# Macaron block on one core: expert weights loaded into the place of their remainders, four row-pair buffers, and norms that keep their intermediates in PSUM

## What is computed

```
x = x + 0.5 * ffn(layernorm(x))          # part 1
x = x + attn(layernorm(x))               # part 2
x = x + 0.5 * ffn(layernorm(x))          # part 3

ffn(x):  logits = x @ W_gate + b_gate;  top 2 of 8 experts
         y = mean over the two of relu(x @ W_e[e] + b_e[e])
attn(x): q, k, v = split(clip(x @ Wqkv.T, -8, 8));  q, k = layer_norm(q), layer_norm(k)
         softmax(q k' / 4 + slopes * distance, causal) @ v @ Wout.T
```

## Time and profile before

| what | value |
|---|---|
| median of three runs | 1060.15 us |
| the profiled execution | 1064.33 us, of which the span of its trace is 1062.6 us |
| PE busy in the span | 876.8 us (83%) |
| DVE busy | 652.9 us (61%) |
| ACT busy | 446.5 us (42%) |
| POOL busy | 352.6 us (33%) |
| moved by DMA | 162.08 MB, 153 GB/s on average |

### The profile page before, as it was taken

One profiled execution on the slowest core, in us unless ns is written; L12 is line 12 of the kernel. 1 busy time (PEld: TensorE's weight loads), 2 busy tenths in 40 slices (PEclk: granted clock), 3 DMA queues, 4 the chain that ended last, 5 costly groups with the idle time before them and its releaser, 6 DMA issues. The chain is left out here.

```text
span 1062.6 us, 20207 instructions
## 1 busy us (share of the span) xinstructions
PE 876.8 (83%) x6688; PEld 646.4 (61%) x6689; DVE 652.9 (61%) x1296; ACT 446.5 (42%) x818; POOL 352.6 (33%) x342
## 2 busy tenths in 40 slices
PE   2667699994698888858999999999859974699994
PEld 2556588873576776635555555555447763588873
DVE  6647244431988887757777777777427667344432
ACT  2332233331244343335777777777723430133321
POOL 4550577764022122120000000000024440577764
PEclk9997799997799999967999999999978995799998
DMA  8784578773244479664666666655148872378773
GB/s 247 268 276 119 165 142 153 140 134 50 82 152 150 154 194 207 179 203 103 145 134 140 132 138 133 140 132 112 33 140 264 292 246 99 85 142 154 135 136 52
DMA packets 112859, 162.08 MB, mean 153 GB/s; under 512 B 16864, under 2 KB 74336, under 8 KB 112512
## 3 DMA queue, kind: packets, MB, share of 16 engines
q1 hardware_dynamic: 94928, 123.85, 42.4%
q0 software_dynamic: 17856, 37.25, 19.1%
HBM read 97.44 MB, written 67.37 MB: 155 GB/s over the span
## 5 line engine op out<-in xcount | busy, mean ns | idle before, releaser
L827 DVE TENSOR_REDUCE att_part<-att_s_ps 128x2 f32<-128x1024 f32 (+2 forms) x160 | 195.4, 1225 | 61.4 <-PE att_s_ps L675 60.9
L789 ACT ACTIVATE att_prob<-att_st_ps 128x512 f32<-128x512 f32 x320 | 173.7, 595 | 78.7 <-PE att_st_ps L701 78.7
L143 PE MATMUL exp_z_ps<-ex_w_hi,exp_xT_hi 128*128 x312 | 131.7, 422 | 2.3 <-issue 1.0
L145 PE MATMUL exp_z_ps<-ex_w_hi,exp_xT_lo 128*128 x312 | 125.7, 403 | 0.0
L144 PE MATMUL exp_z_ps<-ex_w_lo,exp_xT_hi 128*128 x312 | 125.3, 402 | 0.0
L1470 DVE TENSOR_TENSOR exp_xT_lo<-exp_t_ps,exp_xT_hi 128x512 fp32r<-128x512 f32 x78 | 53.9, 692 | 106.7 <-ACT exp_xT_hi L1456 106.7
L1463 ACT ACTIVATE exp_y<-exp_y 128x512 f32<-128x512 f32 x72 | 45.5, 632 | 171.8 <-DVE exp_y L1482 171.8
L1099 POOL TENSOR_TENSOR ex_w_lo<-ex_bias,ex_w_hi 128x1024 fp32r<-128x1024 f32 x32 | 77.0, 2409 | 92.6 <-ACT ex_w_hi L1203 92.4
L1398 POOL DMA_INDIRECT exp_xg<-xn,ex_token_of x78 | 78.2, 1002 | 88.1 <-SPq L1370 60.4
L714 PE MATMUL att_pv_ps<-att_prob,att_v_sb 128*32 128x256 f32 (+2 forms) x1280 | 101.4, 391 | 1.8 <-ACT att_oT L794 1.8
L639 POOL CAST att_m_parts<-att_part 128x28 fp32r<-128x28 f32 x32 | 6.6, 208 | 271.3 <-DVE att_part L831 271.3
(11 more groups left out here) (199 smaller groups left out, 1713.4 us busy)
## 6 DMA issues: line engine op xcount, KB each, us to landing
ex_bias<-in_L_ffn_W_e SPq DMA_DIRECT2D x32, 512.0 KB, 6.8
v_vals<-st_vals SPq DMA_DIRECT2D x16, 512.0 KB, 2.8
...
```

The costliest lines, as they stand in the source:

```text
L143: nc.tensor.matmul(out, x_hi[:, s], w_hi(c), start=(c == 0), stop=False)
L145: last = nc.tensor.matmul(out, x_lo[:, s], w_hi(c), start=False, stop=(c == C - 1))
L789: nc.scalar.activation(prob[n % 2][:, col:col + 512], st_ps[(e + half) % 3][:, :], ACT.Exp).then_inc(exp_done, 1)
L827: nc.vector.tensor_reduce(out, src, X_AXIS, ALU.max, negate=True).then_inc(red_done, 1)
```

## The change

- `load_weights` now writes each piece straight into its place in `ex.w_lo`. ACT rounds from there into `ex.w_hi`, and POOL subtracts in place. There are eight semaphores for the pieces; piece n waits only for ACT to have rounded piece n-8.
- The memory of the two stage buffers becomes two more row-pair buffers (`XR = 4`). Row pair u waits for pair u-4 to be normed and stored. The turned q/k/v weight uses the first two of them, and waits for their rows instead of for POOL.
- SP issues row pairs two ahead and weights up to two pieces further ahead than before.
- ACT rounds the last piece after the last two tiles' copies, not between them and the ones before. POOL subtracts the last piece only once `picked_done` is there, that is after the top-2 selection.
- `rsqrt_steps` keeps its two intermediates in PSUM (`route_ps` in the routes, a bank of its own, `root_ps`, in the q/k/v block) and forms each Newton step as `(v*y)*(-0.5)*y`, so that no operation of it has two inputs in SBUF.

```
 def rsqrt_steps(nc, chain, var, y, bank):
+    n = var.shape[-1]
+    v, t = bank[:, 0:n], bank[:, n:2 * n]
+    chain(nc.vector.tensor_scalar(v, var, EPS, None, ALU.add))
+    chain(nc.vector.tensor_scalar(y.bitcast(I32), v.bitcast(I32), -0.5, 1597463007.0, ALU.mult, ALU.add))
     for _ in range(3):
-        chain(nc.vector.tensor_tensor(tmp[0], y, y, ALU.mult))
-        chain(nc.vector.scalar_tensor_tensor(tmp[0], tmp[0], -0.5, tmp[1], ALU.mult, ALU.mult))
-        chain(nc.vector.scalar_tensor_tensor(y, tmp[0], 1.5, y, ALU.add, ALU.mult))
+        chain(nc.vector.tensor_tensor(t, v, y, ALU.mult))
+        chain(nc.vector.scalar_tensor_tensor(t, t, -0.5, y, ALU.mult, ALU.mult))
+        chain(nc.vector.scalar_tensor_tensor(y, t, 1.5, y, ALU.add, ALU.mult))
...
             def load_x(u):
-                p = u % 2
-                if u >= 2:
-                    sp.wait_ge(xn_done, 2 * u - 2)
-                    sp.wait_ge(x_stored[p], 16 * (u // 2))
+                if u >= XR:
+                    sp.wait_ge(xn_done, 2 * (u - XR) + 2)
+                    sp.wait_ge(x_stored[u % XR], 16 * (u // XR))
...
             def load_weights(n):
-                if n >= 2:
-                    sp.wait_ge(w_lo_done, n - 1)
-                sp.dma_start(w_stage[n % 2][:, :, :], w_e[n // 2, :, :]...
+                if n >= WR:
+                    sp.wait_ge(w_hi_done, n - WR + 1)
+                sp.dma_start(ex.w_lo[:, 2 * n:2 * n + 2, :].bitcast(F32), w_e[n // 2, :, :]...
...
             for n in range(TILES):
                 pool.wait_ge(w_hi_done, n + 1)
-                nc.gpsimd.tensor_tensor(ex.w_lo[:, 2 * n:2 * n + 2, :], w_stage[n % 2][:, :, :],
+                if n == TILES - 1:
+                    pool.wait_ge(picked_done, 1)
+                nc.gpsimd.tensor_tensor(ex.w_lo[:, 2 * n:2 * n + 2, :], ex.w_lo[:, 2 * n:2 * n + 2, :].bitcast(F32),
...
-                if u < PAIRS:
+                if u < PAIRS - 1:
                     weights(2 * u + 1)
+            weights(TILES - 1)
```

More of the change, by code:

```diff
@@ L94, in layernorm_steps @@
     chain(nc.vector.bn_aggr(ln["mv"], ln["stats"]))
-    rsqrt_steps(nc, chain, ln["mv"][:, 1:2], ln["rstd"], (ln["t0"], ln["t1"]))
+    rsqrt_steps(nc, chain, ln["mv"][:, 1:2], ln["rstd"], ln["bank"])
     return nc.vector.tensor_scalar(out, x, ln["mv"][:, 0:1], ln["rstd"], ALU.subtract, ALU.mult)
@@ L223, in qkv_block @@
         parts, vals = st.parts, st.vals
-        ln = m.ln()
+        root_ps = m.ps("root_ps")
+        ln = m.ln(root_ps[:, 8:10])
         stats3 = m.sb("stats3", [P, 3, 6])
         mv3 = m.sb("mv3", [P, 3, 2])
-        rstd3, tmp3a, tmp3b = (m.sb(n, [P, 3]) for n in ("rstd3", "tmp3a", "tmp3b"))
+        rstd3 = m.sb("rstd3", [P, 3])
         o_ps = [m.ps(f"o_ps{i}") for i in range(3)]
@@ L464, in unit @@
                     chain(nc.vector.bn_aggr(mv3[:, s, :], stats3[:, s, :]), apart=(s < (2 if ahead else 1)))
-                rsqrt_steps(nc, chain, mv3[:, :, 1], rstd3[:, :], (tmp3a[:, :], tmp3b[:, :]))
+                rsqrt_steps(nc, chain, mv3[:, :, 1], rstd3[:, :], root_ps[:, 0:6])
                 if ahead:
@@ L905, in route_block @@
         m = Memory(nc, ctx, prefix)
-        w_stage, x = ([ex.bias[:, (2 * k + i) * 2 * D:(2 * k + i + 1) * 2 * D].rearrange("p (c n) -> p c n", c=2)
-                       for i in range(2)] for k in range(2))
+        XR, WR = 4, 8
+        x = [ex.bias[:, i * 2 * D:(i + 1) * 2 * D].rearrange("p (c n) -> p c n", c=2) for i in range(XR)]
+        w_stage = x
         g_raw = m.sb("g_raw", [P, C, E])
@@ L914, in route_block @@
         stats, mv = m.sb("stats", [P, 2, 6]), m.sb("mv", [P, 2, 2])
-        rstd, tmp_a, tmp_b = (m.sb(n, [P, 2]) for n in ("rstd", "tmp_a", "tmp_b"))
+        rstd = m.sb("rstd", [P, 2])
         t_ps = [m.ps(f"t_ps{i}") for i in range(2)]
@@ L978, in route_block @@
         begin_f = m.sb("begin_f", [1, TAB, 1])
-        w_loaded = [m.sem(f"w_loaded{i}") for i in range(2)]
+        w_loaded = [m.sem(f"w_loaded{i}") for i in range(WR)]
         w_hi_done, w_lo_done = m.sem("w_hi_done"), m.sem("w_lo_done")
@@ L983, in route_block @@
         zeroed, ident_done, const_done = m.sem("zeroed"), m.sem("ident_done"), m.sem("const_done")
-        x_loaded = [m.sem(f"x_loaded{i}") for i in range(2)]
-        x_stored = [m.sem(f"x_stored{i}") for i in range(2)]
+        x_loaded = [m.sem(f"x_loaded{i}") for i in range(XR)]
+        x_stored = [m.sem(f"x_stored{i}") for i in range(XR)]
         xn_stored = [m.sem(f"xn_stored{i}") for i in range(2)]
@@ L1040, in _ @@
                 load_o(3)
+            load_x(1)
+            load_weights(0)
+            load_weights(1)
             for u in range(PAIRS):
-                load_weights(2 * u)
-                if u + 1 < PAIRS:
-                    load_x(u + 1)
+                if u + 2 < PAIRS:
+                    load_x(u + 2)
                 if u >= 1:
                     store_xn(u - 1)
-                load_weights(2 * u + 1)
+                if u + 1 < PAIRS:
+                    load_weights(2 * u + 2)
+                    load_weights(2 * u + 3)
                 if proj and 2 * u + 4 < TILES:
@@ L1068, in _ @@
                 sp.wait_ge(wq_tr, 2 * WQ_PAIRS)
-            for par in range(2):
-                sp.wait_ge(x_stored[par], 16 * (PAIRS // 2))
+            for i in range(XR):
+                sp.wait_ge(x_stored[i], 16 * (PAIRS // XR))
             sp.wait_ge(xn_done, TILES)
-            sp.wait_ge(w_lo_done, TILES)
             sp.dma_start(ex.bias[:, :], b_e.rearrange("(a e) h -> a (e h)", a=1).to_broadcast([P, E * D])).then_inc(ex.bias_loaded, 16)
@@ L1201, in weights @@
             def weights(n):
-                act.wait_ge(w_loaded[n % 2], 16 * (n // 2 + 1))
-                nc.scalar.activation(ex.w_hi[:, 2 * n:2 * n + 2, :], w_stage[n % 2][:, :, :], ACT.Copy).then_inc(w_hi_done, 1)
+                act.wait_ge(w_loaded[n % WR], 16 * (n // WR + 1))
+                nc.scalar.activation(ex.w_hi[:, 2 * n:2 * n + 2, :], ex.w_lo[:, 2 * n:2 * n + 2, :].bitcast(F32),
+                                     ACT.Copy).then_inc(w_hi_done, 1)
             if proj:
@@ L1242, in add_x @@
             def add_x(t):
-                row = x[t // 2 % 2][:, t % 2, :]
+                row = x[t // 2 % XR][:, t % 2, :]
                 dve.wait_ge(y_done, t + 1)
@@ L1271, in _ @@
                     norm(nc.vector.bn_aggr(mv[:, k, :], stats[:, k, :]))
-                rsqrt_steps(nc, norm, mv[:, :, 1], rstd[:, :], (tmp_a[:, :], tmp_b[:, :]))
+                rsqrt_steps(nc, norm, mv[:, :, 1], rstd[:, :], route_ps[:, 0:4])
                 if u >= 2:
```

30 lines of the change are left out of this document (14 added, 16 removed).

## The result

The changed kernel takes 1021.72 us (median of 4 runs, 1019.34 to 1027.31) against 1060.47 for the kernel before (4 runs, 1060.13 to 1063.36): ratio 0.963, 95% interval 0.9603 to 0.9658. It gains 38.7 us. The forecast was 1031, a gain of 29, with 1015 to 1047 around it. The profiled execution of the changed kernel is its slowest, 1027.31 us, with a span of 1025.6. So 37.0 us of span can be followed from one trace to the other. Of the executions behind the experiments two ran far slower than the rest (2750.92 us of the kernel before, 1120.69 us of o_first); they are left out of the ratios, but not of the medians.

The account below looks back on a forecast made before the run. No engine bounds the whole span; DVE, stalled by POOL, paces q/k/v, and late loads hold the routes. Route 1 -13.5, q/k/v -10 and route 2 -6 sum to -29.5: 1034.8, less 4.18 gives 1031 us, range 1015 to 1047.

Parts of the forecast that it names:

- the rival in which PE bounds the q/k/v block: q/k/v block: POOL's subtraction falls into a gap, 9.93 us a step, -19 instead of -10, total 1022; chance 0.13.
- The dear link: Norm chains: each of ten links reading PSUM costs 0.055 us more, 12 us in all, total 1043; chance 0.10.
- the slower case: Norm chains: a link nearly doubles; 0.12 us more erases the gain, 0.16 more gives 1070; chance 0.04.
- no release: Norm links: L82 or links with one SBUF input still held by POOL, q/k/v gains nothing, total 1046; chance 0.06.
- Route 1, -14 to the logits: Route 1: pairs at 7.7 us bring the logits from 82.62 to 68.5 us; bounds -18 and -8 after the last-piece cost.
- DVE's floor: Route 1: 5.06 us a pair without stalls, 7.1 with POOL stalling `xn`, 7.4 if the whole 2.35 is paid.
- The DMA floor: Route 1: five transfers a pair at 1.6 us each, 8.1 us, perhaps falling to 6.5 with more loads queued.
- The last piece, +0.6: Route 1's end: POOL's last subtraction after `picked_done` delays DVE operations with two SBUF inputs, costing 0.6 us.
- q/k/v, -10: q/k/v block: one stall instead of two, nine steps at 10.6 gain 6.7, four late ones 3.2; bounds -5 and -19.
- Route 2, -6: Route 2: loads gain 4.5, the last `xn` stall 2.03, POOL's overlap costs 0.6; bounds 0 and -10.
- The last stall (-2.0): Route 2: the last `xn` pair loses its stall of 2.03 us because POOL's last piece is held back.
- the -4.5 for loads: Route 2: of the time estimated as lost waiting for loads, 4.5 us would go.

Follow-up runs that it names:

- o_first: Changed kernel with q/k/v row loads issued earlier, POOL's subtractions in halves, and route 2's attention-output loads ahead of the weight pieces: 1012.88 us, ratio 0.9506.
- yy_sbuf: Changed kernel with v kept in SBUF and y squared from two SBUF inputs into PSUM: 1053.3 us, ratio 0.9887 to the kernel before.
- old_tail: Changed kernel with the last piece as before: ACT rounds it ahead of the last copies, POOL subtracts at once; 1028.45 us, ratio 0.9655.
- halves: Changed kernel with each POOL subtraction split in two halves, in both routes and the q/k/v block: 1021.25 us, ratio 0.9621.
- early_rows: Changed kernel with the row loads in the last eight q/k/v steps issued ahead of the attention block's loads: 1017.87 us, ratio 0.9573.
- The two experiments: Kernel before with only the links moved to PSUM, 1049.79 us; changed kernel with the links' intermediates back in SBUF, 1056.97 us.

## Why the prediction was right, and where its terms were off

- **The number.** The measured 1021.72 lies outside the forecast's own 1026 to 1038 and on the 1022 of the rival in which PE bounds the q/k/v block. That is a coincidence: that rival wanted -19 there, and the block gave -12.3. The 9 us beyond the forecast came from route 1, from the q/k/v block and from the stages that the sum held at nothing.
- **What bounds the stages.** Right. Links read from PSUM run through, no link exceeds 0.17 us, and the stalls that are left lie where the prediction put them: on L1289 in the routes, on L470 and L474 in the q/k/v block. The price of a link in PSUM is -0.01 to 0.01 us (0.16 to 0.17 us, against 0.16 to 0.17 in SBUF, and the medians of yy_sbuf). The dear link (0.055 us more) and the slower case (0.12) are refuted, and so is "no release": L82, from SBUF to PSUM, stays at 165 ns. That rival's price of 1046 was too low as well: with L82, L83 and L85 exposed, yy_sbuf takes 1053.3, since the stalls also eat most of route 1's gain. The Trainium skill (VectorE: DVE Perf Modes, "The TRN2 errata") would have a PSUM source cost 65 ns more, and the rows do not show it.
- **Route 1, -14 to the logits.** Measured -17.1. DVE's floor was right: 7.1 to 7.4 a pair was given for the first six, 7.27 measured. The last pair was to take 5.06, since POOL would have nothing left, and takes 6.01. The DMA floor was mis-sized. It was 1.6 us a transfer and 8.1 a pair, and I took 7.7 between the two floors, where DVE's alone counted. The step that failed is "0.79 of 82 us is 64.8 us of full engines". A share of 0.79 moved 257 GB/s, but 1.03 moves 419, and in proportion it would be 335. By these numbers the share also counts time in which little moves, so it is no measure of the room that is left. A transfer takes 1.25 us here, and the floor is 6.3 for five. Of the 3.0 us missed, 1.6 are the seven pairs and 0.46 the first norm. The 1.5 allowed for the first transfers did not come. The tail took 6.3 instead of 5.7. The logits at 65.5 are thus ahead of the 67 to 70 named as a sign. A bound was also summed wrongly: at 6.6 us a pair the sum gives -20, not -18.
- **The last piece, +0.6.** It did not come as described, and holding the piece back gained nothing that old_tail could show. POOL ran from 71.12 to 73.47, and DVE took its next row up at 73.55. Where POOL's last piece does reach into DVE's rows, in halves, it costs 0.4:

```profile
66.38 2.50 POOL L1114 TENSOR_TENSOR ex_w_lo<-ex_w_lo,ex_w_hi 128x512 fp32r<-128x512 f32 x2 [12.48 <-DVE route_pair L1321]
...
68.33 0.57 DVE L1325 TENSOR_TENSOR route_counts<-route_totals 128x8 f32<-128x8 f32 x1
```

- **q/k/v, -10.** Measured -12.3, of which the 13 steps give 152.5 - 141.5 = 11.0. The mechanism, one stall where there were two, is what the trace shows. The nine steps take 10.2 on average, not 10.6, and give 10.1 instead of 6.7. The four late steps give 0.9 instead of 3.2: their rows wait behind SP's queue, not for a buffer, and a faster DVE only waits longer (9.1 us instead of 6.9). The two misses partly cancel. The other 1.3 lie behind the last `qkv_xn`, where I had counted no gain from the last links. PE became no bound, since the stall moves between `normk` and `qkv_xn`.
- **Route 2, -6.** Measured -2.7, and -5.3 in early_rows, where the code is the same. The last stall (-2.0) went, but not for the reason given: in old_tail, where POOL's last piece is not held back, the last pair has no such stall either. The step that failed is the -4.5 for loads. The eight norms were (872.80 - 802.60) = 70.2 us apart in all and are 70.6 now. From PE's first product with `Wout` to its last, before and after:

```profile
787.30:868.60 81.30, 76.04 (x394) 63.05 (x395) 53.14 (x150) 29.79 (x42) 33.59 (x15) 0.90 0.85 278
755.70:835.50 79.80, 75.20 (x392) 62.74 (x393) 54.78 (x151) 28.68 (x42) 35.84 (x15) 0.91 0.83 289
```

  PE stood idle for only 5.3 us of this before and stands for 4.6 now. Its waits for `route_o` were 1.5 us, twice, and are 2.7, once. So there were no 4.5 us to win from loads. Between the first and the last norm the clock is at 1.2 GHz for some 10 us in both kernels, in two stretches of some 7 and 3.4 us before and in three of 3 to 4 us between 770 and 833 now, so the mean clock in route 2 stays at 0.87. I had read the distance to PE's pace of 9.62 as waiting for loads. A large part of it was the clock, with its means of 0.69 and 0.84 in two stretches of 10 us behind the first norm, in the kernel before:

```profile
802.60:812.60 10.00, 8.77 (x39) 7.19 (x38) 7.84 (x23) 3.58 (x5) 2.74 (x2) 0.69 0.76 240
812.60:822.60 10.00, 9.70 (x53) 8.09 (x52) 7.12 (x21) 4.03 (x6) 4.38 (x2) 0.84 0.93 293
```

  The first norm comes 1.6 us earlier in the stage, and some 0.5 is lost behind the last.
- **That the parts add.** The sum gave route 1's gain to loads and links together, and so held the interaction. The two experiments show how large it is: by themselves they would have promised 24.4 us, not 37.0.
- **The sum.** The three stages give -32.1 against the -29.5 forecast. The other 4.9 us of span are in the stages that the sum held at nothing, within what they vary by. The sum's chains are 32, where the trace has 34 (16 in the routes, 18 in the q/k/v block); that changes nothing, since a link was put at 0. The medians' 38.7 includes that the profiled run of the changed kernel was its slowest.
